# Head attention: the products with V made once per chunk of keys, 512 queries wide, in place of twice, 256 wide

## The reference

```python
qm = q.reshape(d_batch * NB_HEADS, q_len, d_head)
km = k.reshape(d_batch * NB_HEADS, q_len, d_head)
vm = v.reshape(d_batch * NB_HEADS, q_len, d_head)
att = jax.nn.softmax(jnp.einsum('nqd,nkd->nqk', qm, km), axis=-1)
att_out = jnp.einsum('nqk,nkd->nqd', att + batch_pos, vm)
```

## Time and profile before

| | us |
|---|---|
| Median of 3 runs (lowest, highest) | 3153.45 (3146.46, 3154.41) |
| Profiled execution, own time | 3127.85 |
| Its span, first to last instruction | 3126.0 |
| PE busy | 2871.7 (92%) |
| DVE busy | 2131.5 (68%) |
| ACT busy | 1797.5 (58%) |

### The profile page before, as it was taken

How to read it: one execution, slowest core, us unless ns; L and a number is a source line. 1 busy time by engine, 2 the same in 40 slices (tenths; PEclk the granted TensorE clock), 3 DMA queues, 4 the chain that set the end, 5 groups by cost and what they waited for, 6 DMA issues and landing times. The chain is left out here.

```text
span 3126.0 us, 55346 instructions
## 1 busy us (share of the span) xinstructions
PE 2871.7 (92%) x20714; PEld 1749.8 (56%) x20714; DVE 2131.5 (68%) x3332; ACT 1797.5 (58%) x3503; POOL 773.9 (25%) x1336
## 2 busy tenths in 40 slices
PE   5888999996799999999999999999786689899999
PEld 2666888885543333333333333333253367688888
DVE  5445555444689999999999999999044445555554
ACT  3444443334238888888888888888634345433333
POOL 4542310001322222222222222211102555230000
PEclk8999999998769999999999999999887799999999
DMA  8884211106955544445555444442133589321110
GB/s 244 267 275 151 65 40 31 31 23 212 280 62 63 63 51 55 54 59 63 63 63 63 55 55 53 56 55 32 34 132 117 162 280 289 91 65 31 31 31 21
DMA packets 446941, 302.05 MB, mean 97 GB/s; under 512 B 170306, under 2 KB 421286, under 8 KB 446678
## 3 DMA queue, kind: packets, MB, share of 16 engines
q1 hardware_dynamic: 412758, 214.59, 35.2%
q0 software_dynamic: 33920, 83.93, 8.5%
HBM read 183.27 MB, written 118.78 MB: 97 GB/s over the span
## 5 line engine op out<-in xcount | busy, mean ns | idle before, releaser
L1481 DVE TENSOR_REDUCE mx_ha<-s_ps_ha 128x2 f32<-128x1024 f32 x1024 | 1242.9, 1221 | 73.0 <-PE s_ps_ha L1388 65.8
L1547 ACT ACTIVATE probs_ha<-s_ps_ha 128x512 f32<-128x512 f32 x2048 | 1108.8, 595 | 192.1 <-PE s_ps_ha L1399 57.9
L1388 PE MATMUL s_ps_ha<-ks_ha,qs_ha 48*128 48x512 f32 x2048 | 759.0, 454 | 20.7 <-DMA ks_ha<-parts_d 15.5
L1399 PE MATMUL s_ps_ha<-qs_ha,ks_ha 50*128 50x512 f32 x2048 | 749.5, 446 | 0.8 <-ACT probs_ha L1547 0.2
L1410 PE MATMUL o_ps_ha<-probs_ha,vs_ha 128*32 128x256 f32 (+1 forms) x7936 | 646.7, 398 | 0.9 <-DVE oT_ha L1508 0.9
L1388 PEld LDWEIGHTS s_ps_ha<-ks_ha,qs_ha 48*128 48x128 f32 x2048 | 312.6, 190 | 452.2 <-DVE mx_ha L1481 372.6
L858 ACT ACTIVATE probsT_a<-pT_ps_a 128x512 fp32r<-128x512 f32 x256 | 146.4, 597 | 424.3 <-PE pT_ps_a L732 424.3
L1410 PEld LDWEIGHTS o_ps_ha<-probs_ha,vs_ha 128*32 128x32 f32 x7936 | 156.5, 108 | 359.7 <-issue 185.9
L1399 PEld LDWEIGHTS s_ps_ha<-qs_ha,ks_ha 50*128 50x128 f32 x2048 | 304.6, 185 | 33.0 <-ACT probs_ha L1547 32.6
L1339 POOL TENSOR_TENSOR onorm_ha<-oT_ha,rinv_ha 128x256 f32<-128x256 f32 x32 | 19.9, 621 | 981.6 <-DVE rinv_ha L1511 981.6
L775 DVE TENSOR_REDUCE nmax_a<-s_ps_a 128x1 f32<-128x2048 f32 x64 | 146.7, 2292 | 163.0 <-PE s_ps_a L721 163.0
(11 more groups left out here) (202 smaller groups left out, 3863.7 us busy)
## 6 DMA issues: line engine op xcount, KB each, us to landing
xs_p<-xs_d SPq DMA_DIRECT2D x282, 128.0 KB
ys_d<-y_p SPq DMA_DIRECT2D x66, 512.0 KB, 3.8
qs_ha<-parts_d SPq DMA_DIRECT2D x192, 128.0 KB, 6.1
ks_ha<-parts_d SPq DMA_DIRECT2D x192, 128.0 KB, 7.1
parts_d<-parts_hp POOLq DMA_DIRECT2D x32, 512.0 KB, 5.0
leaf_w_p<-in_wa SPq DMA_DIRECT2D x6, 1048.0 KB
leaf_w_p<-in_wb SPq DMA_DIRECT2D x6, 1040.0 KB
xs_d<-y_p SPq DMA_DIRECT2D x6, 1024.0 KB, 12.8
```

The costliest lines, as they stand in the source:

```text
L1388: nc.tensor.matmul(s1_ps[:, e % BANKS, :], qs[0:QKROWS, n % SLOTS, c, :], ks[0:QKROWS, n % SLOTS, g * 4:(g + 1) * 4, :].rearrange("p c t - ...
L1399: nc.tensor.matmul(out, ks[LOW:LOW + KR, n % SLOTS, c, :], qs[LOW:LOW + KR, n % SLOTS, g * 4:(g + 1) * 4, :].rearrange("p c t -> p (c t)") ...
L1481: nc.vector.reduce_max(mx[:, at:at + 2], s1_ps[:, e % BANKS:e % BANKS + 2, :], AX_X).then_inc(s1_free, 1)
L1547: nc.scalar.activation(probs[:, (n + c) % (LATE + 1), g * 512:(g + 1) * 512], s2_ps[:, turn % TURNS, :], ACT.Exp).then_inc(s2_free, 1)
```

## The change

`products` loses its argument `half`, always takes 512 columns, and is called once per chunk, behind k = 1. The constant `HALF` and the second call in the last loop go. Buffers, semaphores and the programs of DVE, ACT, POOL and SP stay the same.

```diff
-            def products(n, c, half):
-                if half == 0:
-                    pe.wait_ge(s2_free, turn_of["score", n, QG * c + QG - 1] + 1)
-                elif c == 0:
-                    return
-                at, size = (0, 512) if c == 0 else (half * HALF, HALF)
+            def products(n, c):
+                pe.wait_ge(s2_free, turn_of["score", n, QG * c + QG - 1] + 1)
                 for g in range(QG):
-                    last = nc.tensor.matmul(o_ps[g * COLS:(g + 1) * COLS, at:at + size], vs[:, n % SLOTS, c, :],
-                                            probs[:, (n + c) % (LATE + 1), g * 512 + at:g * 512 + at + size],
-                                            start=(c == 0), stop=(c == RC - 1 and half == 1), tile_position=(0, g * COLS))
-                if c == RC - 1 and half == 1:
+                    last = nc.tensor.matmul(o_ps[g * COLS:(g + 1) * COLS, :], vs[:, n % SLOTS, c, :],
+                                            probs[:, (n + c) % (LATE + 1), g * 512:(g + 1) * 512],
+                                            start=(c == 0), stop=(c == RC - 1), tile_position=(0, g * COLS))
+                if c == RC - 1:
                     last.then_inc(o_made, 1)
...
                         score(n, c, k)
-                        if k % 2 == 0:
+                        if k != 1:
                             continue
                         if c >= LATE:
-                            if c == LATE and k == 1 and n > 0:
+                            if c == LATE and n > 0:
                                 pe.wait_ge(turn_step, 2 * n - 1)
-                            products(n, c - LATE, k // 2)
+                            products(n, c - LATE)
                         elif n > 0:
-                            products(n - 1, RC + c - LATE, k // 2)
+                            products(n - 1, RC + c - LATE)
```

More of the change, by code:

```diff
@@ L1167, in head_attend @@
         QUADS = P // COLS
-        HALF = 512 // 2
         W = B * DH
@@ L1472, in _ @@
             for c in range(RC - LATE, RC):
-                for half in range(2):
-                    products(BLOCKS - 1, c, half)
+                products(BLOCKS - 1, c)
         @block.vector
```

## The result

| us | before | after |
|---|---|---|
| Median | 3153.93 (4 runs) | 3229.4 (4 runs) |
| Ratio of the two, 95% interval | | 1.0235 (1.022 to 1.0249) |
| Span of the profiled execution | 3126.0 | 3226.4 |
| Block, from first position matmul to the next | 41.83 | 44.12 |
| First products to end of the last, head attention | 1328.99 | 1402.35 |

The blocks cost 73.4 us more (1402.35 - 1328.99); the prediction's sum was 74. The spans differ by 100, not by 74. The other 27 us lie outside the changed stage: the first products start 12.1 us later (927.34 against 915.26), and from the last ones to the end of the span it is 15.0 us more (896.7 against 881.7). The medians differ by 75.5, as the blocks do.

The account below looks back on a forecast made before the run. PE sets the pace in head attention, DVE 5% behind. Blocks at +2.29 us give +66.4 over 29 periods; the later parts add +2.9, +2.5 and +2.3; +74 on 3153.45 makes 3227 us, range 3210 to 3245.

Parts of the forecast that it names:

- the prediction's sum: Extra time over all head attention blocks and the chunks at the end: +74 us.
- The ring: Fourth score in a row waits for k2's exponential to free its bank: products 2.64 us apart in place of 2.467.
- The wait in every chunk: PE's weight load at k1' waits for ACT about 0.46 us, some 480 times in place of 30, over 200 us.
- The adding whole: A 512-wide product adding onto `o_ps` takes 0.99 us to the next pair; bounds 0.95 and 1.14.
- Rival D: The adding whole costs as much as two halves, 1.14 us: +72 us more, 3299 us; chance 0.05.
- The positions: Chunk across a block's position matmuls takes 4.52 us from products to products, 4.66 before, without a wait at k1'.
- The block: One head attention block takes 4.52 + 15 x 2.64 = 44.12 us, +2.29 us.
- The median: Median of the whole kernel: 3153.45 + 74 = 3227 us, the difference put on the median.
- Rival A: Faster: PE's work shrinks to 2.12 us a chunk and ACT keeps up, -44 us, 3109 us; chance 0.08.
- Rival B: No change: the next chunk pays back the loss at k1', average near 2.47 us, 3153 to 3162 us; chance 0.03.
- Rival C: Granted clock falls to half in one chunk in ten of the blocks: 77 us, together 3304 us; chance 0.04.
- DVE's idle time: DVE idle ahead of its reductions by 0.2 us per chunk, some 110 us in place of 73.

Follow-up runs that it names:

- run 3: Changed kernel with every second scan left out and 4 banks for scores in place of 3: chunk 2.12 us, block 36.29 us.
- run 4: Changed kernel with exponentials over 256 of 512 queries: chunk 2.43 us, block 41.14 us.
- run 6: Changed kernel with exponentials over 256 of 512 queries and maxima over 256 of 512 columns: chunk 2.42 us, block 40.90 us.
- run 5: Changed kernel with DVE's maxima over 256 of every 512 columns: chunk 2.64 us, block 44.10 us.
- run 1: Changed kernel with products in two halves of 256, both behind k1: chunk 2.64 to 2.65 us, block 44.18 us, one execution 3199.5 us.
- version 10: Kernel before with a block's first products made in two halves: ratio 0.9976, block 41.56 us.
- version 11: Kernel before with a block's first products in halves and its last whole, ahead of the next block's position matmuls: ratio 0.9974, block 41.52 us.
- the pieces of 384: Changed kernel, all work done, with products in pieces of 384 queries behind every third score: ratio 1.0348, block 45.50 us.
- run 7: Changed kernel, all work done, with 4 banks for scores and 3 for scans, DVE reducing one bank at a time: chunk 2.70 us, block 45.07 us.

## Why the prediction was right

- *The ring.* 0.57 + 0.65 + 0.43 + 0.99 = 2.64 was read off one place in the block of before. It is 2.64 in every usual chunk after. Its cause (a bank short), its latency of ACT, and its indifference to DVE were each shown: by run 3, by runs 4 and 6, and by run 5.
- *The wait in every chunk.* Right: 447 times, 15 in each of 30 blocks (a few records are missing). But each is 0.37 us on average and not 0.46, 165 us in these blocks and 202 in the whole of head attention (33 there before). In most chunks DVE holds the scan of k0' a little (0.07 us at 1043.63), which also bares its weight load, so that less of the ring shows as ACT's. The length of the chunk doesn't feel it: with the maxima cut, every one of the waits is the full 0.46, and the chunk is 2.64 all the same.
- *The adding whole.* Taken at 0.99, bounds 0.95 and 1.14; it measured 0.99 (1042.00 to 1042.99). Rival D falls, and run 1 gives two halves in a row 1.00.
- *The positions.* 4.52 us, as worked out.
- *The block.* 44.12 predicted, 44.12 measured. The stage's +73.4 stands against a sum of 74.1. The chunks at the end that have no scans are 2.60 us apart and not 2.64, which makes up the difference.
- *The median.* 3227 against 3229.4. The step to put the difference on the median and not on the profiled time had no row behind it, and it is luck that it held: both kernels were timed while the parts outside the blocks took their longer time. The span of after (3226) lies 26 us over the 3200 forecast for it, and those 27 us lie in parts that the change doesn't touch. The kernel before itself ran at medians of 3125.4, 3153.5 and 3127.9 us beside the three sets of experiments, about as far apart. The ratio doesn't hang on it.
- *Rival A.* It took PE's own shrinking work as the whole of the change. That a change of tiling mode drains TensorE is stated by the Trainium skill, "TensorEngine Tiling (Array Packing)", Key Properties. The rows price it only together with what else lies around the products (0.34 and 0.33 against 0.23). The gain is real, and run 3, with half of the scans, shows its full size, 2.11 us a chunk; three banks keep it from showing.
- *Rival B.* The loss isn't paid back by the next chunk: products stand 2.63 to 2.65 us apart one after the other.
- *Rival C.* The clock stayed at 1.00 in the blocks, from 927 to 2330 us. The granted clock of before isn't at 9 tenths in all of head attention, as the text ahead of the prediction has it: it is 0.56 from 845 to 900 us and 0.54 from 900 to 915, ahead of the first products, and 1.00 from there on. So low levels do occur beside this stage, and in it neither kernel meets one.
- *Smaller misses.* DVE's idle time was put at 110 us and is 169: two reductions in a row take 2.35 us (1043.76), not 2.44, which is 0.09 a chunk or some 40 of the 59 us; the rest is not traced. The product matmuls number 4096, not 3970, for chunk 0 had been whole already.

Open: the 0.003 us by which half chunks differ between versions 10 and 11. Not tried: a fourth bank for scores without taking it from the scans. All eight banks are in use (4 for scans, 3 for scores, 1 for `o_ps`).

## What to carry to other kernels

When work is gathered into larger pieces, write down what now stands in a row on the in-order engine, and compare that run with the number of buffers it turns through: n buffers carry n items in a row, and item n+1 can't start before the consumer has freed the first one's buffer, here 0.57 + 0.65 = 1.22 us after that one started. Look for a place in the old program where the new order already occurs, a block's beginning or end; its rows give the new period before anything is built. A fix for one ring has to be held against every other buffer on the same queue, as the pieces of 384 show, and as the fourth bank taken from the scans shows even more plainly: there the same ring came back through DVE.

## What the runs showed of the hardware

- Four banks of 512 take DVE 2.48 us as four reductions (run 7, 1310.71) and 2.35 as two reductions of two banks each (after, 1043.76): taking pairs saves 5%.
- The weight load of a score that has to wait for its bank starts with its matmul (before, 1042.97); one that hasn't starts ahead of it (before, load 1040.21, matmul 1040.43). From the first kind of score to the products it is 0.43 us, from the second 0.33.
- An exponential of 128x512 frees its bank for the next score 0.65 us after its start (before, 1042.32 to 1042.97), one of 128x256 0.44 (run 6). What the producer waits for is this latency, with ACT idle for 1.07 us of each chunk in run 6.
- PE waits for ACT in every chunk of after, and the granted clock is 1.00 over the whole stage.
